# Causal mask of the second layer's scores: one addition over four heads, then one row maximum per token tile

## What is computed

```python
scale = 1.0 / np.sqrt(HEAD_DIM).astype(np.float32)
attn = jnp.einsum('bqhd,bkhd->bhqk', q, k) * scale
causal = jnp.tril(jnp.ones((S, S), dtype=bool))
attn = jnp.where(causal, attn, jnp.float32(-jnp.inf))
attn = jax.nn.softmax(attn, axis=-1)
out = jnp.einsum('bhqk,bkhd->bqhd', attn, v).reshape(B, S, C)
return out @ wo.T
```

## Time and profile before

| | us |
|---|---|
| median of 3 runs | 3479.36 |
| lowest, highest of the runs | 3472.05, 3519.74 |
| the profiled execution | 3471.18 |
| its span in the trace | 3469.4 |
| TensorE busy over the span | 3041.3 (88%) |
| VectorE busy | 2184.6 (63%) |
| ScalarE busy | 1498.4 (43%) |
| GpSimd busy | 1166.1 (34%) |

### The profile page before, as it was taken

The page is one execution under the profiler, slowest core; times in us unless marked ns, Lnnn a source line. Parts: engine busy times, 40 slices in busy tenths (PEclk is TensorE's granted clock), DMA queues, the critical chain, the costliest instruction groups (busy, mean ns, idle before and its releaser), DMA issues.

```text
span 3469.4 us, 86074 instructions
## 1 busy us (share of the span) xinstructions
PE 3041.3 (88%) x34622; PEld 2100.7 (61%) x34622; DVE 2184.6 (63%) x5540; ACT 1498.4 (43%) x3474; POOL 1166.1 (34%) x995
## 2 busy tenths in 40 slices
PE   5699998999988988988688898776899999999988
PEld 5377666767766666666577677663454554554554
DVE  7467688676777676785366554465456656656554
ACT  1645555554544555552256421153353343343231
POOL 0324445643445344444055164422121221220110
PEclk7899899998989999996799999898899999999989
DMA  7101211311213212113487443574111111111000
GB/s 247 47 32 57 67 51 60 111 48 46 67 53 97 68 52 63 58 58 99 135 218 192 127 122 116 185 245 118 41 28 49 43 31 49 44 31 43 1 19 19
DMA packets 224087, 280.83 MB, mean 81 GB/s; under 512 B 35072, under 2 KB 172464, under 8 KB 223312
## 3 DMA queue, kind: packets, MB, share of 16 engines
q1 hardware_dynamic: 184448, 216.93, 19.3%
q0 software_dynamic: 34896, 54.20, 7.0%
q10 hardware_dynamic: 4352, 4.20, 0.3%
HBM read 184.64 MB, written 90.62 MB: 79 GB/s over the span
## 4 chain that ended last, share of the span: by engine, by line
PE 65%; DVE 14%; issue 6%; POOL 5%; ACT 4%; DMA 3%; DVEq 0%; ACTq 0%; SPq 0%; POOLq 0%
PE banks L3079 6%; PE banks L576 5%; PE banks L2614 3%; PE banks L1965 3%; PE banks L825 3%; PE banks L2600 2%; PE banks L1974 2%; PE banks L2626 2%; PE banks L812 2%; PE banks L1307 2%; PE banks L2870 2%; PE banks L2780 2%; PE banks L607 2%; PE banks L2153 2%; PE banks L2166 2%
## 5 line engine op out<-in xcount | busy, mean ns | idle before, releaser
L576 PE MATMUL banks<-s_d_xT,s_w_qkvg 128*128 128x512 f32 x640 | 322.1, 628 | 10.2 <-DVE s_d_kq L674 6.9
L2742 ACT ACTIVATE s_g_pT<-banks 128x1536 f32<-128x1536 f32 (+1 forms) x96 | 152.8, 1592 | 364.0 <-PE banks L2616 364.0
L699 POOL TENSOR_TENSOR s_d_kq<-s_d_kq,s_d_far 128x509 f32<-128x509 f32 x128 | 170.2, 1331 | 222.0 <-DVE s_d_kq L674 221.7
L3079 PE MATMUL banks<-s_m_we,s_m_tT 128*128 128x512 f32 x512 | 234.5, 603 | 6.0 <-DVE s_m_x L3142 6.0
L674 DVE SCALAR_TENSOR_TENSOR s_d_kq<-banks,s_conv_w,s_d_kq 128x511 f32<-128x511 f32 (+1 forms) x256 | 190.3, 744 | 43.2 <-ACT s_d_far L626 38.4
L1965 PE MATMUL banks<-s_q_xsT,s_q_w 128*128 x1008 | 160.1, 282 | 39.6 <-issue 30.8
L2699 DVE TENSOR_REDUCE s_g_off<-banks 128x4 f32<-128x512 f32 (+2 forms) x96 | 117.2, 1220 | 123.1 <-PE banks L2600 121.0
L1965 PEld LDWEIGHTS banks<-s_q_xsT,s_q_w 128*128 128x128 f32 x1008 | 153.8, 196 | 62.7 <-issue 50.5
L576 PEld LDWEIGHTS banks<-s_d_xT,s_w_qkvg 128*128 128x128 f32 x640 | 116.3, 195 | 105.1 <-issue 81.8
L825 PEld LDWEIGHTS banks<-s_d_TB,s_d_XT 32*32 32x32 f32 x9216 | 110.2, 111 | 98.2 <-issue 71.3
L652 ACT ACTIVATE s_d_square<-banks 128x128 bf16<-128x128 f32 x512 | 134.5, 279 | 77.7 <-PE banks L607 76.9
(11 more groups left out here) (421 smaller groups left out, 7920.4 us busy)
## 6 DMA issues: line engine op xcount, KB each, us to landing
s_q_w<-w12p SPq DMA_DIRECT2D x128, 257.0 KB, 6.1
s_q_xs<-xs SPq DMA_DIRECT2D x32, 516.0 KB, 6.0
s_d_E<-sums SPq DMA_DIRECT2D x64, 256.0 KB
s_r_xT<-xfT SPq DMA_DIRECT2D x12, 1024.0 KB
tree<-s_r_bias SPq DMA_DIRECT2D x96, 128.0 KB
s_r_work<-xf SPq DMA_DIRECT2D x24, 512.0 KB, 4.2
og<-s_d_o SPq DMA_DIRECT2D x16, 512.0 KB, 3.0
sorted<-s_q_acc SPq DMA_DIRECT2D x32, 256.0 KB, 2.1
```

The costliest lines, as they stand in the source:

```text
L576: ins = e.matmul(bk[6 + j % 2][:], w[:, par, c, self.COL[what] + h * P:self.COL[what] + (h + 1) * P], xT[:, c, :], start=(c == 0), stop=(c ...
L699: e.tensor_tensor(d[:, 3:], d[:, 3:], self.far[:, j % 2, 3:], ALU.add).then_inc(self.tapped, 1)
L2742: e.activation(self.pT[c][:], psum[:, 0:4, 0:self.COLUMNS[c]], ACT.Exp).then_inc(self.exped, 1)
L3079: ins = e.matmul(self.product_bank(b, k, q)[:], self.tT[:, c, t * P:(t + 1) * P], self.we[:, c, (2 * half + q) * 512:(2 * half + q + 1) * ...
```

## The change

For each unit, one `tensor_tensor` adds the mask to the diagonal blocks of all four heads in place in PSUM: 4 heads times 128 columns for units 1 and 2, and 4 heads times 2 tiles times 128 columns (1024 per partition) for unit 0. It raises a new semaphore, `masked`. VectorE waits for it, and then takes, per tile, one `tensor_reduce` over the whole row of (t+1)*128 columns for all four heads, straight into four columns of `nmax`. The tile `off` and its semaphore go. The counts of `scored`, `maxed` and `max_turned` stay as they were.

```diff
-        self.off, self.off_made = sb("g_off", [P, TPB, 4]), g.sem("second_off_made")
+        self.masked = g.sem("second_masked")
...
-                    for t, a in units:
-                        if t:
-                            e.tensor_reduce(self.off[:, t, :], psum[:, 0:4, a:a + t * P], AX.X, ALU.max).then_inc(self.off_made, 1)
-                    for t, a in units:
-                        if t:
-                            e.wait_ge(self.off_made, 3 * (m + 1) + t)
-                        for k in range(4):
-                            block = g.bank[k][:, a + t * P:a + (t + 1) * P]
-                            lower = self.off[:, t, k:k + 1] if t else -1e30
-                            ins = e.tensor_tensor_reduce(block, block, g.neglb[:], 1.0, lower, ALU.add, ALU.max, self.nmax[:, t, 32 * k + 16:32 * k + 17])
-                        ins.then_inc(self.maxed, 1)
+                    if c == 0:
+                        diagonal = psum[:, 0:4, :].rearrange("p k (x n) -> p k x n", n=256)[:, :, :, 0:P]
+                        e.tensor_tensor(diagonal, diagonal, g.neglb[:, None, None, :].broadcast_to((P, 4, 2, P)), ALU.add).then_inc(self.masked, 1)
+                    else:
+                        t, a = units[0]
+                        diagonal = psum[:, 0:4, a + t * P:a + (t + 1) * P]
+                        e.tensor_tensor(diagonal, diagonal, g.neglb[:, None, :].broadcast_to((P, 4, P)), ALU.add).then_inc(self.masked, 1)
+                    e.wait_ge(self.masked, 3 * (m + 1) + c + 1)
+                    for t, a in units:
+                        e.tensor_reduce(self.nmax[:, t, :].rearrange("p (k n) -> p k n", n=32)[:, :, 16], psum[:, 0:4, a:a + (t + 1) * P], AX.X, ALU.max).then_inc(self.maxed, 1)
```

## The result

| | before | after |
|---|---|---|
| median, 20 runs of each | 3480.23 us | 3498.09 us |
| lowest to highest | 3449.17 to 3519.74 | 3469.88 to 3512.07 |
| ratio after / before, 95% interval | | 1.0054 (1.0034 to 1.0073) |
| profiled execution, span | 3469.4 us | 3502.5 us |
| VectorE busy, instructions | 2184.6 us, 5540 | 2195.4 us, 4644 |

The change makes the kernel slower by 0.5%, some 19 us: small, but the interval lies clear of 1. Forecast were +5 us.

The account below looks back on a forecast made before the run. TensorE was taken to set the second layer's pace, VectorE counting only by latency. Unit 0's waits +4.6 us and the others -0.3 gave +4.3: 3471.2 to 3475.5 profiled, plus 8.2 to the median, 3484; range 3462 to 3508 us.

Parts of the forecast that it names:

- 3479 to 3489: Whole kernel: forecast time in us with the third rival in it, chance 0.76, likeliest 3484.
- the rival of half the rate: Units' mask additions into PSUM run at half rate, 1024 elements costing 1.07 us more: +39, 3518 us; chance 0.06.
- My own elapsed sum: VectorE's three units, first start to last end: 8.56 against 8.31 us a round, 8 us more over 32 rounds.
- The rival by busy time: Units' maxima: busy time counts, so unit 0 shortens by about 1 us, waits lose 15 us: 3464; chance 0.16.
- The rounds whose unit 0 had no wait have room: Second layer, unit 0: rounds without a TensorE wait absorb the 0.29 us delay; one checked had 0.7 us.
- The sum: TensorE's waits for maxima: 16 of unit 0 grow +4.6 us, the other 13 shrink -0.3, together +4.3 us.
- The third rival: Work behind unit 0 in VectorE's list starts some 0.3 us later; TensorE waiting each round: 10 us, 3489.
- The reserve at the other end: Lengthened TensorE waits let ScalarE and GpSimd catch up, so later waits shrink by as much: 3479 us.

Follow-up runs that it names:

- The extra instruction in the kernel before: Kernel before plus a useless reduction over 208 elements ahead of unit 0's maxima in every round: 3495.18 against 3482.27 us, ratio 1.0027.
- the unit 0 exchange: Changed kernel with unit 0 in the old form, ratio 0.9996; then only unit 0 in the new form, units 1 and 2 old, ratio 1.0028.
- unit 0 as after: Unit 0 in the changed form, units 1 and 2 as in the kernel before: 3494.13 against 3482.27 us, ratio 1.0028.
- the two with the extra instruction in these rounds: Kernel before plus a useless reduction ahead of unit 0's maxima, in all rounds (ratio 1.0027) or only in rounds beginning a sequence (1.0008).
- The kernel without the mask: Kernel before with the mask left out of the maxima of tiles 1 to 3, kept in tile 0: ratio 0.9976, a second time 1.0003.

## Why the prediction was right in kind and short in size

- **The number.** 3498 against a likeliest 3484: the rise is 18.8 us in place of 5. It lies outside 3479 to 3489, which had the chance of 0.76, and inside the range to 3508 only because that range was widened for the spread of three runs. No mechanism of the prediction gives 3498, so that it falls into the range is luck.
- **TensorE sets the pace, and VectorE's work counts by its latency.** Right. The extra instruction in the kernel before (ratio 1.0027) and the unit 0 exchange (0.9996 and 1.0028) show it.
- **The costs of the instructions.** Right within 0.01 us: 0.694, 1.229 and 2.293 us against 0.69, 1.22 and 2.29. The addition into PSUM takes what one into SBUF does (0.694 and 0.687 us for 512 elements), so the rival of half the rate is out. Unit 0 takes 3.08 us as said. TensorE's waits for the maxima were forecast at about 42 us and are 44.3.
- **VectorE's busy time.** Wrong. I said that it would fall by 62 us. It rose by 10.8 (2184.6 to 2195.4). I had added the rows' durations, and rows that overlap count once in the engine's busy time. My own elapsed sum, 8 us more, was the right forecast of that number, and the two statements stood in one paragraph.
- **The rival by busy time.** Out. The saving of 2 us a round that it needs did not exist. The start times 0.27 us apart for instructions of 0.36 us spoke against it, and the result bears them out. By one sentence of the Trainium skill's VectorE: DVE Perf Modes (The DRAIN you can't avoid), that the next operation does not start until the pipe empties, the saving would have existed; the same section adds that one that is not held starts earlier, which the prediction left out and which these rows show. The Trainium skill's Perfetto Trace Analysis (Optimizing Scalar/DVE Operations), by which the write acknowledgement overlaps with the next instruction, agrees with them.
- **Which rounds pay.** Here a step failed: "The rounds whose unit 0 had no wait have room". The one checked has 0.7 us, and of the 16 units 0 without a listed wait 11 have 0.7 us or more. The other five have none. In one of them the kernel before has these rows, TensorE and then VectorE:

```profile
2710.82 2.89 PE L2870 MATMUL banks<-s_l_va,s_l_sT 128*128 128x65 f32 x24
2713.82 1.14 PE L2614 MATMUL banks<-s_g_qkT 17*128 17x512 f32 x8
```

```profile
2713.53 0.14 DVE L2706 DVE_READ_ACCUMULATOR2_ANT s_g_nmax<- 128x1 f32 x1
```

  The maxima end at 2713.67 and TensorE starts 0.15 us later, exactly the lag of the rounds with a wait (2870.38 to 2870.53). TensorE had stood since 2710.82 + 2.89 = 2713.71, a wait of 0.1 us, too short to be listed: there was no room at all. In the changed kernel these five have waits of 0.40 to 0.42 us, and 20 units 0 wait in place of 16: 20 x 0.30 = 6.1 us where I had 16 x 0.29 = 4.6.
- **The clock.** Missing altogether, and the larger of the two errors. The sum took a wait to cost its own length. In the three traces of each kernel about half of what the layer grew, 6 to 7 of 12.8 us, is what TensorE lost at the lower clock.
- **The third rival**, another wait coming in for 10 us, did not show: TensorE's waits for the experts' sums, which stand behind unit 0's, grew from 6.0 to 6.6 us, and no other by more than 0.1.
- **The reserve at the other end** (later waits shrink by as much: 3479) did not show: TensorE's waits for ScalarE stayed at 9.4 and 5.7 us before and after.

**What stays open.** What makes the clock fall in one execution and not in the next. At the beginning of a sequence, falls came in 22 of 30 places in the kernels with the wait of 1.4 us there (after three times, unit 0 as after, and the two with the extra instruction in these rounds) and in 11 of 30 in those with 1.1 us. The kernel without the mask, with a wait of 0.5 us there, had none in 10. So falls go with the length of the wait. But one kernel of the first kind had 2 of 5 and two of the second had 3 of 5, and the kernel without the mask also ran at a lower mean clock. That the longer wait raises the chance is likely; that it alone decides is not shown. The traces add up to 12.8 us of the measured 18.8 (11.8 to 25.4 by the interval); the rest is within the uncertainty of three traces each.

## What to carry to other kernels

Before merging small instructions, read their start times and not their durations: back to back they overlap, and a few long instructions of which one must wait for the other can end later than nine short ones. On a chain that a busy engine waits for, an unlisted wait isn't room; take the distance between the releasing instruction's end and the waiting one's start, and compare it with the lag of the rounds that do wait. Here a longer wait of TensorE cost more than its length, since its granted clock fell more often behind it.

## What the runs showed of the hardware

- A VectorE addition with its input and result in PSUM and a bf16 operand broadcast over heads takes 694 ns for 512 elements and 1229 for 1024; one from PSUM into SBUF takes 687 for 512.
- VectorE instructions that wait for nothing overlap: masked maxima with rows of 0.36 us start 0.27 us apart. One that waits for the instruction before it starts 0.03 us after that one's whole row (2628.17 + 1.23 to 2629.43).
- In the second layer TensorE's clock fell to its lower level for 3.4 us behind waits of 1.38 and 1.15 us, and at times behind 1.07 and 1.10; with dense matmuls behind it, a fall cost 1.7 us. With the falls taken off, 21 rounds of one kernel repeat within 0.4 us from trace to trace. Much of the spread between executions of one kernel on one chip, 3461 to 3508 us, goes with the mean granted clock (0.917 to 0.937, 24 us per 0.01).
- The same program took 3480 us on some chips and 3584 to 3606 on another. Nearly all of the difference lies in the first layer (second layer 1081.7 us on one, 1076.3 and 1086.7 on the other), and it goes with the clock there: the first layer had a mean granted clock of 0.91 on the one and of 0.88 on the other. What lowers it isn't shown.
